# A fused attention and int8 feed-forward layer: where the end-of-pair work stands in the issue order, and the cap on steps per attention unit

## The reference

```
xn = _layernorm(x, axis=-1)
s = _L0_attn_ref(xn, L0_attn_qkv_weights)          # 16 heads of 64, causal
g = _silu(_L0_ffn_ref(xn, L0_ffn_weight_q, L0_ffn_weight_scale, L0_ffn_bias))
x = x + s * g
```

## Time and profile before

| what | value |
|---|---|
| median of 2 runs | 1582.39 us (1581.05 to 1583.74) |
| the profiled execution, its own time | 1583.47 us |
| its span on the slowest core (core 7) | 1581.9 us |
| spans of the 8 cores | 1562.9 to 1581.9 us |
| mean granted TensorE clock of the 8 cores | 0.795 to 0.816 of full |
| TensorE busy (core 7) | 1129.4 us, 71% |
| ScalarE busy | 719.4 us, 45% |
| VectorE busy | 573.4 us, 36% |
| GpSimd busy | 300.1 us, 19% |

### The profile page before, as it was taken

One profiled execution on the slowest core, in us unless ns is written; L12 is line 12 of the kernel. 1 busy time (PEld: TensorE's weight loads), 2 busy tenths in 40 slices (PEclk: granted clock), 3 DMA queues, 4 the chain that ended last, 5 costly groups with the idle time before them and its releaser, 6 DMA issues.

```text
span 1581.9 us, 17864 instructions; the slowest of 8 cores (1562.9 to 1581.9 us)
## 1 busy us (share of the span) xinstructions
PE 1129.4 (71%) x5200; PEld 466.9 (30%) x5200; DVE 573.4 (36%) x1086; ACT 719.4 (45%) x905; POOL 300.1 (19%) x412
## 2 busy tenths in 40 slices
PE   0346546445464558997987887888798888888886
PEld 0112212212221214443443333333233333333332
DVE  0484382562825553227237227222721011100000
ACT  0121220211211213454454465467447778788876
POOL 1440330412504541122022022011200000000000
PEclk9956757659565665865987998988898999899998
DMA  7110010100101211121011011001000000000000
GB/s 117 47 34 14 20 34 0 34 20 6 48 0 54 60 54 40 41 67 51 10 48 40 8 40 61 7 21 41 21 8 21 14 14 14 15 27 14 8 14 13
DMA packets 24463, 47.46 MB, mean 30 GB/s; under 512 B 4272, under 2 KB 7472, under 8 KB 24368
## 3 DMA queue, kind: packets, MB, share of 16 engines
q0 software_dynamic: 8816, 20.98, 5.4%
q1 hardware_dynamic: 15552, 25.34, 5.3%
HBM read 40.54 MB, written 8.39 MB: 31 GB/s over the span
## 4 chain that ended last, share of the span: by engine, by line
PE 35%; DVE 26%; ACT 19%; issue 8%; POOL 5%; DMA 5%; DVEq 1%; ACTq 0%; POOLq 0%; SPq 0%
ACT eT L774 16%; PE Oa L788 4%; PE pm L551 4%; PE pm L534 4%; PE Ob L792 3%; DVE t_r L430 3%; DVE t_b L433 3%; DMA xst<-x 3%; PE pm L581 3%; PE sT L729 2%; DMA w8n<-w 2%; DVE t_g L428 2%; PE pm L842 2%; PE pm L846 2%; DVE bnst L240 2%
## 5 line engine op out<-in xcount | busy, mean ns | idle before, releaser
L774 ACT ACTIVATE eT<-sT 128x1024 bf16<-128x1024 f32 (+1 forms) x576 | 549.0, 953 | 278.7 <-PE sT L735 144.9
L788 PE MATMUL Oa<-eT,v_aug 128*65 128x512 bf16 (+1 forms) x576 | 242.8, 422 | 2.5
L792 PE MATMUL Ob<-eT,v_aug 128*65 128x512 bf16 (+1 forms) x576 | 230.6, 405 | 0.0
L729 PE MATMUL sT<-qT,kTa 64*128 64x512 bf16 x448 | 183.9, 419 | 39.6 <-ACT eT L774 38.1
L735 PE MATMUL sT<-qT,kTa 64*128 64x512 bf16 x448 | 186.7, 425 | 0.0
L891 POOL DMA_DIRECT2D out<-outs x32 | 24.4, 764 | 756.3 <-DVE outs L884 656.4
L827 DVE TENSOR_TENSOR wpr<-Oa,gT 64x512 bf16<-64x512 f32 x32 | 21.9, 683 | 395.4 <-PE Ob L792 394.5
L301 PE MATMUL sT<-Wqk,xnK 128*128 128x512 bf16 x256 | 111.6, 615 | 47.3 <-ACT xnK L289 42.8
L729 PEld LDWEIGHTS sT<-qT,kTa 64*128 64x128 bf16 x448 | 40.4, 94 | 228.5 <-issue 226.1
L788 PEld LDWEIGHTS Oa<-eT,v_aug 128*65 128x65 bf16 x576 | 68.3, 119 | 106.9 <-issue 95.7
L551 PE MATMUL pm<-Wv,xnq 128*128 128x512 bf16 x256 | 74.5, 443 | 23.7 <-DVE v_aug L558 19.4
(11 more groups left out here) (122 smaller groups left out, 1608.5 us busy)
## 6 DMA issues: line engine op xcount, KB each, us to landing
xst<-x SPq DMA_DIRECT2D x96, 256.0 KB, 2.9
xres<-xr POOLq DMA_DIRECT2D x32, 256.0 KB, 3.6
out<-outs POOLq DMA_DIRECT2D x32, 256.0 KB, 2.8
Wqk<-wq POOLq DMA_DIRECT2D x1, 1024.0 KB, 14.8
Wqk<-wk POOLq DMA_DIRECT2D x1, 1024.0 KB, 25.7
Wv<-wv POOLq DMA_DIRECT2D x1, 1024.0 KB, 30.4
w8n<-w POOLq DMA_DIRECT2D x4, 256.0 KB, 2.6
wscb<-wsc SPq DMA_DIRECT2D x4, 0.5 KB, 5.6
```

What stands on the lines that cost most here:

```text
L729: t.matmul(sT[par][:, o:o + w], kTa[0:64, P, 128 * jb:128 * jb + 128], qT[P][0:64, qb + o:qb + o + w], start=True, stop=True), waits=w0)
L774: s.activation(eT[pe3][:].rearrange("p (b n) -> p b n", b=2)[:, :, o:o + w], sT[par][:].rearrange("p (b n) -> p b n", b=2)[:, :, o:o + w], ...
L788: sc.emit("tensor", lambda t: t.matmul(Oa[:, o:o + w], v_aug[:, jb, 65 * hA:65 * hA + 65], eT[pe3][:, o:o + w], start=(jb == 0), stop=(jb ...
L792: c_av = sc.emit("tensor", lambda t: t.matmul(Ob[:, o:o + w], v_aug[:, jb, 65 * hB:65 * hB + 65], eT[pe3][:, 512 + o:512 + o + w], start=( ...
```

## The change

Two edits. In the unit loop the call that issues the next closure of `att["pend_gate"]` moves from the head of the unit (ahead of the held-back value matmuls and the scores) to behind the unit's exponential; whether it is issued is still decided at the head. In `pump()` the upper limit of 3 on `budget` goes.

```diff
@@ -711,9 +711,7 @@
             for jb in range(njb):
                 if P == 0 and jb == 4 * c - 1:
                     drain_pre()
-                if att["pend_gate"] and jb in pops_at:
-                    close_open()
-                    att["pend_gate"].pop(0)()
+                do_pop = att["pend_gate"] and jb in pops_at
                 if jb >= 3:
                     flush_av()
                 par = att["unit"] % 2
@@ -777,6 +775,9 @@
                     AF.Exp),
                     waits=(("pe", c_sc), ("pe", att["eT_rd"][pe3])), inc="ac")
                 att["sT_rd"][par] = c_ex
+                if do_pop:
+                    close_open()
+                    att["pend_gate"].pop(0)()
                 avw = [("ac", c_ex), ("dv", dep["v"][jb // 4])]
                 hA, hB = 2 * P, 2 * P + 1
 
@@ -1041,7 +1042,7 @@
             uc["u"] += 1
             left = max(1, nunits - uc["u"] + 1)
             needed = max(0, dlA - ia["k"]) + (len(ib["lst"]) - ib["k"] + 1) // 2
-            budget = max(1, min(3, -(-needed // left)))
+            budget = max(1, -(-needed // left))
             for _ in range(budget):
                 if ib["k"] < len(ib["lst"]) and ia["k"] >= ib["gate"]:
                     stepB()
```

## The result

The changed kernel takes 1627.24 us (median of 11 runs, 1621.16 to 1634.89); the kernel before, run beside it on the same chip, takes 1578.91 us (10 runs). The ratio is 1.030, with a 95% interval from 1.027 to 1.033, which is +43 to +52 us, 47.5 in the middle. The forecast was +39 us, 1621 us from a kernel before of 1582.4 us, with a range up to 1640.

The account below looks back on a forecast made before the run. No single engine bounds the whole: TensorE's queue limits chunk 0, ScalarE sets chunk 7's pace between borders. Terms 21 + 4 + 0 + 14 = +39 us give 1622.5 us, or 1621 against the median 1582.4; range 1590 to 1640.

Parts of the forecast that it names:

- The cap on the budget: In `pump()`: the quotient is never above 1, so the limit of 3 never acts; cost 0.
- Steps 1 to 5: Clean border: first exponential 1.03 us earlier, copies 1.45 later, small matmuls behind them, exponential of unit 3 0.89 late.
- the term of 21 us: Delay at the 21 borders without projection matmuls in units 0 and 1, at 1.0 us each; 19 to 24.
- The clock at clean borders: Longer spell at 1.2 GHz at 10 of 21 clean borders, 1.4 us each: +14 us; bounds 0 and 29.
- the 1.4 us of the earlier trace: Chunk 7's first two pairs: 39.1 us at clock 0.96, 40.5 at 0.92; taken as a longer low spell's price.
- Chunk 0: Three borders: copies 2.3 us later, scores of unit 1 taken out; 3 x 1.2 = +4 us, 0 to 7.
- Projection borders: Seven borders with projection matmuls in units 0 and 1: one gap closes, another opens; 0 us, -6 to +8.
- Step 6: Clean border: four transposes move behind unit 4's scores, TensorE stays busy; price 0, at most some 0.4 us regained.
- Delay without the clock: Rival: steps 1 to 6 hold, but chunk 7's granted clock stays at 0.94; 1607 us, chance 20%.
- Clock lost at every border: Rival: all 21 clean borders get the longer spell at 1.2 GHz; 1636 us, chance 9%.
- ScalarE decides and the kernel is faster: Rival: ScalarE paces late chunks, its first exponential comes 1.03 us earlier, 22 us won; 1561 us, chance 6%.
- Nothing to be seen: Rival: the delay is made up within the pair, TensorE needing 0.88 us per unit against ScalarE's 1.12; chance 5%.

## Why the prediction was right, and where its terms were off

**The cap on the budget.** The price of 0 is right. The changed kernel with the limit of 3 put back builds the same program, byte for byte, so the whole difference is the moved calls'.

**Steps 1 to 5, the order at a clean border.** Counted from the end of the last exponential of the old pair: the first exponential was forecast at 0.90 us and is at 0.90; the small matmuls at 3.54, measured 3.53; the exponential of unit 2 at 4.50, measured 4.49, where it had been at 4.48. So the 1.03 us won by the first exponential is indeed used up before unit 2, and everything behind the small matmuls is late. In length, the three late pairs whose time at 1.2 GHz did not grow lost 1.1, 0.8 and 1.1 us: the 1.0 us of the forecast. With fillers in both kernels it is 0.7, in the ten pairs of chunks 2 to 5 it is 0.9. So the term of 21 us measured 15 to 21.

**The clock at clean borders.** The mechanism was right. What the 1.4 us of the earlier trace rows priced is a low spell of 6.8 instead of 3.4 us (medians of those two pairs before); the border of the earlier trace rows had a short one too. In late pairs (6,1), (6,2), (7,0) and (7,2) the time at 1.2 GHz grew by 3.4 us and the pair by 2.1 to 2.7; less the delay that is 1.1 to 1.7 each, around the 1.4 of the earlier trace rows. That is four or five of eight borders, near the 10 of 21. What was mis-sized is chunk 1. Its three clean pairs lost 3.7, 3.8 and 4.1 us by the medians of each pair, with 7.9 to 9.5 us more at 1.2 GHz each, and 9.1 us by the median of the cores' sums, where my price per border gives at most 3 x 2.4 = 7.2. The 1.4 us came from pairs with 32 units, in which the clock recovers after the border; a pair of chunk 1 has 8 units, and in the changed kernel two of the three stand at 1.2 GHz for their whole 18.6 us. Less the delay of 1 us, each microsecond more at 1.2 GHz cost 0.3 us in chunk 1 and 0.3 to 0.5 in the late pairs: what was mis-sized is the time at the lower clock, not its rate. I carried a price per border from long pairs to short ones. The ten clean pairs of chunks 2 to 5 are the other side: they lost 9.4 us, 0.9 a border, and their time at 1.2 GHz did not grow in sum, which leaves the delay alone (the sum is good to about 3 us). All 21 clean pairs lost 21.3 + 13.9 = 35.2 us against 21 + 14 = 35 forecast. That these meet to 0.2 us is luck: the delay is known as 15 to 20 us, the clock's part as the rest, and it falls on other borders than an even share of 10 in 21 says.

**Chunk 0.** Its three pairs lost 3.4 us against 4 forecast (0.9, 1.5 and 1.2). It runs at 1.2 GHz either way (32.7 us of 36.2).

**Projection borders.** Forecast 0 with bounds -6 and +8, measured +6.8 in the changed kernel (+3.8 in its version with fillers in chunks 6 and 7) and +2.1 when only they are changed. Nothing here contradicts the local argument of step and counter-step; the bounds were needed for what comes from elsewhere.

**Step 6, the transposes, is the step that failed, within a forecast that held.** It was priced at 0 because TensorE stays busy either way. That holds in the late chunks it was argued from, and not in chunks 1 to 5, where the kernel with this move alone is 11 us slower. I had read one late timeline for it and no short pair. Since the moves are not additive, how much of those 11 us is in the 47.5 can't be said.

**The rivals.** Delay without the clock (1607 us) falls: the time at 1.2 GHz grew in the clean and late pairs, and fillers that lower it give the time back. Clock lost at every border (1636 us) is near in size, but three of the eight late borders, and in sum the ten clean ones of chunks 2 to 5, got no more time at 1.2 GHz. ScalarE decides and the kernel is faster (1561 us) falls: the scores of unit 3 come at 1455.01, 6.63 us after the border's start, where they would have had to be there by 5.1 (at a border at full clock they come at 5.9). The first exponential came 1.03 us earlier, and ScalarE then stood idle for 1.88 us ahead of that of unit 3, where there had been no gap. The Trainium skill's advice to take the engine with the highest occupancy (Perfetto Trace Analysis, Identifying the Most-Contended Engine) and look for its gaps (the same page, Optimization Strategy), read as the prediction reads it, points to this change; the runs show it 3.0% slower. Adding 40 matmuls in TensorE's waits made the kernel 0.7% shorter. The Trainium skill's rule to issue matmuls back to back in batches (Perfetto Trace Analysis, Matmul Optimizations) agrees with that. Nothing to be seen (1582 to 1590 us) falls with the result.

**The range.** 1590 to 1640 held the 1627. The increment was forecast 8 us low, 39 against 47.5. In the groups it is 45.4, and of that difference the projection pairs' 6.8 are all, a figure good to 3 us; 2 us more lie outside the pairs measured. The prediction takes a change of about 2% as the least that can be told from none; with 10 and 11 runs the interval here is 0.3% to either side.

## What to carry to other kernels

Where engines replay a fixed order, price a moved call by what it will wait behind and what then waits behind it on each queue, up to the point where the two orders meet again; a gap closed on the busiest engine is worth nothing if the same work stands in its queue a microsecond later. Put short helper work of the other engine (here the copies) where that engine is idle anyway, and keep what TensorE waits for ahead of what it doesn't need yet. Read the price of a clock loss from a stretch as short as the one that it is carried to, and when TensorE has to wait at a border, try both shortening the block that holds its queue and filling the wait with matmuls that nobody needs.

## What the runs showed of the hardware that was not expected

- **A matmul with one row and one column in fp32 is dear.** (Its weights are one row of 128 numbers, what streams through is one number.) Each shows as two records and starts 0.22 us after the one before (1451.91, 1452.13) at 2.4 GHz and 0.43 us at 1.2 GHz; the bf16 form starts every 0.03 us. Eight of them at 32 borders, in bf16 instead, make the kernel 2.8% faster, some 45 us, or 1.4 us a border; by the table 3.5 us a border in chunk 0, where TensorE's queue is the limit, and 1.2 in the late pairs. The weight load of one record takes 0.24 us on average in fp32 and 0.09 us in bf16 (line 846, slowest core of each).
- **Useless matmuls pay.** 40 of them in chunks 6 and 7 win 11 us, because 27 us at 1.2 GHz become full speed. With all 21 clean borders filled beside the bf16 sums, the time at 1.2 GHz in clean pairs falls from 120.0 to 54.8 us and in late ones from 30.7 to 0.0.
- **The clock fell without any long idle time.** In the kernel before it fell at 1414.03, after 1.13 us idle, the small matmuls and the next scores and value matmuls. At the border of the changed kernel shown above TensorE's row reads: 1.11 us idle, a pair of scores, 1.07 us idle, then the small matmuls, of which the last is already at 1.2 GHz.
